# Group 0's top keys chosen, fetched and scored inside the early expert tiles; two sequences' expert sums and their QKV moved one group later

## The reference

```
x = x + haar_attention(ln(x))        # QKV, 3-level Haar transform, product, inverse, output matrix
x = x + ffn(ln(x))                   # "early" routed experts: top 2 of 8, hidden 256, relu^2
x = x + attention(ln(x))             # 16 heads of 8; per head three softmaxes, averaged:
    local : keys with |i - j| <= 128
    top   : the 128 keys with the highest (ln(x) @ Ws.T + bs) for this head
    global: the first 64 keys
x = x + ffn(ln(x))                   # "late" routed experts, same weights
```

## Time and profile before

| | us |
|---|---|
| median of 3 executions | 564.72 |
| profiled execution, its own time | 566.64 |
| its span in the profile | 564.9 |
| PE / DVE / ACT / POOL busy | 489.1 / 380.5 / 350.9 / 235.8 |

### The profile page before, as it was taken

One profiled execution on the slowest core, in us unless ns is written; L12 is line 12 of the kernel. 1 busy time (PEld: TensorE's weight loads), 2 busy tenths in 40 slices (PEclk: granted clock), 3 DMA queues, 4 the chain that ended last, 5 costly groups with the idle time before them and its releaser, 6 DMA issues.

```text
span 564.9 us, 12118 instructions
## 1 busy us (share of the span) xinstructions
PE 489.1 (87%) x3754; PEld 294.7 (52%) x3754; DVE 380.5 (67%) x1442; ACT 350.9 (62%) x835; POOL 235.8 (42%) x312
## 2 busy tenths in 40 slices
PE   7999899867767799997899989899989978789876
PEld 3577667646424344444455544444545423667665
DVE  4876886437777589897797777686888851334325
ACT  7577655766304767667657757577757556567643
POOL 3411164544474452242544245663543242445440
PEclk9999999998779899999999989999999999999989
DMA  7899012746120110000200002111010003656306
GB/s 225 294 358 306 2 42 73 258 171 227 39 63 9 43 45 13 10 15 15 63 19 16 15 14 64 29 26 31 14 33 17 25 31 109 238 168 213 125 15 185
DMA packets 52094, 51.65 MB, mean 91 GB/s; under 512 B 11811, under 2 KB 43689, under 8 KB 52032
## 3 DMA queue, kind: packets, MB, share of 16 engines
q1 hardware_dynamic: 46976, 44.52, 24.4%
q0 software_dynamic: 5056, 6.37, 4.5%
HBM read 12.11 MB, written 22.63 MB: 61 GB/s over the span
## 4 chain that ended last, share of the span: by engine, by line
PE 57%; DVE 18%; issue 10%; ACT 7%; DMA 4%; SPq 2%; another core or an unknown queue 1%; POOL 1%; DVEq 0%; ACTq 0%; POOLq 0%
PE BANK L1889 6%; PE BANK L1953 5%; PE BANK L1978 4%; PE BANK L1925 4%; PE BANK L2061 4%; PE BANK L1857 3%; PE BANK L1845 2%; PE BANK L1981 2%; PE BANK L1930 2%; PE BANK L1984 2%; PE BANK L2192 2%; PE BANK L1948 2%; PE BANK L1794 2%; DVE XN_c L1523 2%; PE BANK L1956 2%
## 5 line engine op out<-in xcount | busy, mean ns | idle before, releaser
L1166 ACT ACTIVATE PT<-BANK 128x256 f32<-128x256 f32 (+2 forms) x352 | 158.1, 492 | 97.0 <-PE BANK L1953 70.9
L746 POOL DMA_INDIRECT GOT<-kv_rows,CHOSEN x64 | 65.5, 1024 | 47.5 <-PE BANK L1953 25.2
L1523 DVE CUSTOM_DVE_ANT_0 XN_c<-BANK,BANDQ 128x384 f32<-128x384 f32 (+1 forms) x128 | 67.8, 530 | 12.4 <-PE BANK L1925 5.2
L1523 DVE CUSTOM_DVE_ANT_0 XN_a<-BANK,BANDQ 128x256 f32<-128x256 f32 (+1 forms) x128 | 56.7, 443 | 21.4 <-PE BANK L1925 17.3
L1528 DVE TENSOR_REDUCE QST<-BANK 128x4 f16<-128x512 f32 x64 | 44.3, 696 | 19.2 <-PE BANK L1930 13.2
L1978 PE MATMUL BANK<-PT,V 128*32 128x256 f32 (+1 forms) x512 | 49.2, 457 | 0.7 <-ACT PT L1166 0.6
L1889 PE MATMUL BANK<-XNT_ALL,W 128*128 128x512 f32 x96 | 46.7, 612 | 0.0
L798 POOL DMA_INDIRECT yt_late<-QKV,IDY_late x31 | 30.4, 980 | 33.6 <-DVE QKV L1388 23.4
L980 ACT ACTIVATE PT<-BANK 128x512 f32<-128x512 f32 x48 | 27.6, 598 | 24.5 <-PE BANK L1889 23.3
L1948 PE MATMUL BANK<-BANDK,IDB 128*128 128x256 bf16 x128 | 36.0, 282 | 7.4 <-ACT PT L1166 5.9
L766 POOL TENSOR_TENSOR SUM<-NRM 128x128 f32<-128x128 f32 x16 | 7.3, 458 | 80.0 <-DVE NRM L1544 79.8
(11 more groups left out here) (369 smaller groups left out, 1249.4 us busy)
## 6 DMA issues: line engine op xcount, KB each, us to landing
xs_late<-W SPq DMA_DIRECT2D x1, 6984.0 KB, 36.4
xs_early<-W SPq DMA_DIRECT2D x1, 4680.0 KB, 16.5
KZB<-W SPq DMA_DIRECT2D x16, 256.0 KB
KZC<-W SPq DMA_DIRECT2D x15, 256.0 KB
kv_rows<-KV SPq DMA_DIRECT2D x4, 768.0 KB
PT<-W SPq DMA_DIRECT2D x11, 256.0 KB
QKV<-xs_late SPq DMA_DIRECT2D x31, 72.0 KB
W<-w SPq DMA_DIRECT2D x2, 1024.0 KB, 8.2
```

What stands on the lines that cost most here:

```text
L746: nc.gpsimd.indirect_dma_start(GOT[g % 2][:, i, :], None, KV_ROWS[g // GROUPS][:, :], bass.IndirectOffsetOnAxis(ap=CHOSEN[:, c:c + 1], axi ...
L1166: nc.scalar.activation(PT[u % PT_RING][:, 0:w], P2_BANK[u % SCORE_RING][:, 0:w], ACT.Exp, scale=SCALE).then_inc(S["exp_done"], 1)
L1523: nc.vector.tensor_tensor_reduce(out=JUNK[v % 2][:, 0:n], in0=P1_BANK[v % SCORE_RING][:, 0:n], in1=BANDQ[:, off:off + n], scale=1.0, scala ...
```

## The change

- **Key choice.** `ROUNDS_TILE` has 5, 3 and again 5 steps a tile instead of 2 and 3, so that all 47 stand at tiles 4 to 15; `turn_orders(0)` and `row_choice(0)` come at tile 16, now through bank 7; `turn_keys(0)` and `chosen_keys(0)` at tile 20.
- **Row numbers for the scatter.** `early_id` leaves DVE; POOL makes each number itself, right before the DMA that uses it, after the wait for `tile_y`.
- **Fetch.** POOL issues group 0's four fetches after tiles 16 and 17, two each, and copies them after tile 18. Group 1's fetch still follows the 23rd tile and the wait for all result DMAs. `global_values(0)` moves ahead of the tiles.
- **SP.** The spreads of groups 0 and 1 are issued in halves after the loads of tiles 14, 15, 17 and 18; the rows of K and V are stored after load 16 instead of load 12; `spread_top(0)` comes before the results' loads.
- **First scores.** 18 of group 0's 22 first-pass units (all but the top ones) stand at tiles 14 to 21. The tiles' result bank is one instead of two (bank 4 is now a score bank). 29 of the 37 fillers go.
- **Moved into the groups.** The adds and statistics of sequences 2 and 3 go to (0, 8) up to (1, 1) (`SUM_C`), `rstd` to POOL's group 1, the normalisations to (1, 4) and (1, 10), their turns and the score of the second key choice from group 0 to group 1, its steps from groups 1 to 5 to groups 2 to 6, its last part from (5, 7) to (6, 13). The eight QKV products, which stood in groups 1, 1, 2, 2, 3, 3, 4 and 6, stand in groups 2, 2, 2, 3, 3, 4, 5 and 6.
- **Group 8.** Its chosen keys are turned at (7, 5) instead of (6, 13), and its first pass has the top units last (as groups 0 and 1), no longer spread. POOL issues its fetches at units 15 to 21 of group 6, and all of group 9's fetch at the start of its group 7.

```diff
-MORE_ROUNDS = {(g, u) for g in range(1, 5) for u in range(0, UNITS, 2)} | {(5, u) for u in (0, 2, 4)}
+MORE_ROUNDS = {(g, u) for g in range(2, 6) for u in range(0, UNITS, 2)} | {(6, u) for u in (0, 2, 4)}
-ROUNDS_TILE = {i: 2 if i < 12 else 3 for i in range(4, NT_EARLY - 1)}
-ROWS_TILE, STORE_TILE = 7, 12
+ROUNDS_TILE = {i: 3 if 7 <= i < 12 else 5 for i in range(4, 16)}
+ROWS_TILE, STORE_TILE = 7, 16
+SPREAD_TILE = {14: (0, 0), 15: (0, 1), 17: (1, 0), 18: (1, 1)}
+ORDERS_TILE, GATHER_TILE, KEYS_TILE = 16, (16, 17), 20
+FIRST_TILE = 14
+SUM_C = {(0, 8): (2, 0), (0, 11): (2, 1), (0, 14): (2, 2), (0, 17): (3, 0), (0, 20): (3, 1), (1, 1): (3, 2)}
-NORMS_C = {(0, 4): 2, (0, 7): 3}
+NORMS_C = {(1, 4): 2, (1, 10): 3}
-SEL_GROUP, SEL_AT = 5, 7
+SEL_GROUP, SEL_AT = 6, 13
+LATE_GATHER = (15, 17, 19, 21)
...
+def first_scores(i):
+    return range(min(TOP_W, 9 * (i - FIRST_TILE) // 4), min(TOP_W, 9 * (i - FIRST_TILE + 1) // 4)) if i >= FIRST_TILE else range(0)
...
-        D_BANK = {"early": BANK[3:5], "late": BANK[3:4]}
+        D_BANK = {"early": BANK[3:4], "late": BANK[3:4]}
...            # POOL, tile_out
                 pool.wait_ge(R[w.tag]["tile_y"], n + 1)
+                i = n if w is EARLY else slot
                 if w is EARLY:
-                    pool.wait_ge(R[w.tag]["tile_id"], n + 1)
+                    nc.gpsimd.tensor_scalar(IDY["early"][:, i:i + 1], XT_IN["early"][n % IN_RING][:, D + 1:D + 2], float(UNUSED), None,
+                                            ALU.add).then_inc(R["early"]["tile_id"], 1)
+                    pool.wait_ge(R["early"]["tile_id"], n + 1)
...            # POOL, the tiles
             for n in range(NT_EARLY):
                 tile_out(EARLY, n)
                 if n == ROWS_TILE:
                     key_rows(0)
+                if n in GATHER_TILE:
+                    half = n - GATHER_TILE[0]
+                    pool.wait_ge(S["sel_done"], 1)
+                    gather(0, range(half * PAIR, (half + 1) * PAIR))
+                elif n == GATHER_TILE[-1] + 1:
+                    gathered(0)
             for slot in range(Y_RING):
                 pool.wait_ge(Y_OUT["early"][slot], 16 * slot_count(EARLY, slot))
-            global_values(0)
-            pool.wait_ge(S["sel_done"], 1)
-            gather(0)
-            gathered(0)
             gather(1)
-            rstd("c", 2)
-            rstd("c", 3)
             gathered(1)
             gather(2)
...            # POOL, at the start of group 7
+                if g - 1 == SEL_GROUP:
+                    gathered(2 * GROUPS)
+                    gather(2 * GROUPS + 1)
+                    gathered(2 * GROUPS + 1)
...            # DVE, the tiles
             for i in range(NT_EARLY):
-                early_id(i)
                 if QKV_TILE <= i < QKV_TILE + T + 1:
                     c_add(1, i - QKV_TILE)
                 picks(0, ROUNDS_TILE.get(i, 0))
-            picks(0, PICKS)
-            both_orders(0)
...
+                if i == ORDERS_TILE - 1:
+                    picks(0, PICKS)
+                    both_orders(0)
+                if i == ORDERS_TILE:
+                    row_choice(0)
+                if i == KEYS_TILE:
+                    chosen_keys(0)
+                maxima(first_scores(i))
...            # PE, the tiles
+                if i == ORDERS_TILE:
+                    turn_orders(0)
+                if i == KEYS_TILE:
+                    turn_keys(0)
+                for w in first_scores(i):
+                    p1(0, w)
```

166 lines of the change are left out of this document (81 added, 85 removed).

## The result

The changed kernel takes 568.12 us (median of 20 runs, 565.54 to 572.7); the kernel before, run beside it, 565.68 (20 runs). The ratio is 1.0053, 95% interval 1.0031 to 1.0075: slower by half a per cent. The forecast was 556.7, and the range up to 564.5 does not hold the time. The profiled execution has 568.62 us, its span 566.8 (564.9).

What follows compares the result with a forecast made beforehand. The groups run at their limit on PE and DVE, so gain lies only before the first groups; -11.5 - 2.5 + 1.5 + 2 + 2.5 = -8.0 us, 556.7 us on the median of 564.7, range 548.5 to 564.5.

Steps and rivals of the forecast that it cites:

- steps 1 to 3: From the key choice to PE's turn of group 1's keys at (0, 2): that turn comes 11.5 us earlier.
- steps 5 to 7: Groups 1 to 7: work moved in and late service of groups 8 and 9 cost +1.5, +2 and +2.5 us.
- step 4: Rest of group 0 after (0, 2): 19.5 us instead of 22.0, -2.5, with DVE the fullest engine.
- Step 1: Key choice at the tiles: both orders written at about 138.8 us instead of 149.0.
- PE's idle stretch: At tile 15: PE idle 3 to 6 us, its fourth first-pass score waiting for DVE's first maximum.
- Step 2: From the choice to group 0: scatters of 1.65 us, group 0 could begin 15.8 us earlier, at 158.9.
- Step 3: At (0, 2): PE waits 4.3 us for group 1's keys, behind four scatters; (0, 2) at 165.3, -11.5 us.
- Rival A: At the tiles: scatters of 2.45 us make POOL the clock; kernel slower, 568.2 us; chance 9%.
- The rule cited from the Trainium skill: Group 0: two-SBUF-input DVE instructions hold off POOL's SBUF reads; four adds cost POOL 1.6 us, at most 2.8.
- B: Rival, in the groups: they hide the work given them, steps 5 to 7 give +1, 551.7 us; chance 18%.
- C: Rival, in the groups: full charge and clock low after each wait, step 4 +1, 561.2 us; chance 14%.
- D: Rival, at the tiles: PE or late loads delay the choice or tile 16 to 144, 562.2 us; chance 9%.

Runs made afterwards that it cites:

- e14: Changed kernel with early tiles' down products alternating between two result banks up to tile 13; ratio to the kernel before 1.0063.
- e11: Changed kernel with row numbers a tile ahead, group 1's fetches before the last four scatters, dense second key choice, two result banks; ratio to the kernel before 0.9845.
- e2: Changed kernel with POOL making each row number one tile ahead of its scatter; ratio to the kernel before 1.0044.
- e6: Changed kernel, unchanged, measured again as reference for the follow-ups; 546.19 us, ratio to the kernel before 1.0087.
- e7: Kernel before with only the late half: work moved into the groups, group 0 still prepared behind the tiles; ratio to the kernel before 1.0027.
- e4: Changed kernel with second key choice dense over (2, 0) to (5, 4), groups 8 and 9 served as before; ratio to the kernel before 1.0018.
- e12: Changed kernel with numbers a tile ahead, group 1's fetches early, dense second choice, ten fillers before group 0's key turn; ratio to the kernel before 0.9866.
- e5: Kernel before the change, unchanged, measured again as reference for the follow-ups; 541.45 us.

## Why the prediction was wrong

The parts first. Up to group 8 the forecast is -8.0 us and the first pair has +5.4. Of these 13.4 us, 6.8 are lost by (0, 2), steps 1 to 3, and 7.2 in groups 1 to 7, steps 5 to 7; step 4 gives 0.5 back.

*Step 1, the choice.* Both orders written at 141.08, forecast 138.8. DVE adds the first QKV product at 121.67 in place of 117.88: 1.2 us of this are the later start of the trace, 2.6 the single bank, which makes PE late. The steps and additions behind it run faster than forecast (three steps in 1.49 us in place of 1.55) and win 1.5 back. What failed is "the scores are in at 110.01, as now" (111.74) and the 0.5 us for the single bank, which moreover is named in the step but not added in its sum. The bank costs 2.3 us of the choice (e14). PE's idle stretch is 3.7 us, at tile 17 and for a load, not for a score at tile 15. That it is harmless was not tried, but e11, the fastest kernel, has 3.93 there.

A reading that was off: the clock line of the earlier trace rows is below 9 in slices 10, 11, 12 and 14, that is from 127 to 169 us and from 184 to 198; slice 13 is at 9. No term of the sum hangs on it.

*Step 2, to group 0.* Forecast -15.8, measured -12.3. CHOSEN is 2.6 late (143.39 against 140.8). The first fetch is late by that and by 0.5 more, since POOL is still at a scatter (143.38 to 144.44), and the keys by 3.9, since two scatters at 2.11 stand between.

*Step 3, the step that failed.* The mechanism stands: PE waits at (0, 2) for group 1's fetch, behind four scatters and the landing of the last. Its size does not: 7.39 us in place of 4.3, and (0, 2) at 172.06, -4.7 in place of -11.5. The mis-sized term is "small operation 0.23, 0.3 until the DMA's start, 1.10: 1.65 us each". I took the 0.3 from DMAs that wait for nothing of POOL's own. It is 0.77, and the scatter 2.11. e2, the kernel with nearly my price (1.63), says what this term is worth. Counted from the dense additions, (0, 2) is 6.9 us earlier than before in e6 and 10.3 in e2, where 11.5 was forecast: 3.4 of the 4.6 us that are missing there. The first pair misses 6.8: 3.9 are there when group 0's keys are in hand (the late choice and two long scatters), four more long scatters add 2.0 and the last one's landing 1.2 (2.05 us of idle time in place of 0.9), and the landing and copies of the fetch give 0.3 back. Rival A had said that a scatter costs from 2.0 us on, and the wait it named is there in small, with a choice at 143 and not POOL at 148. It was given 9% because I tested its price on the operation alone. Its total, 568.2, is next to the measured 568.12 by luck: it had step 3 at 0 (measured -4.7) and groups 1 to 7 at +6 (measured +13.2).

What none of my steps saw: the late half by itself wins 10 us up to group 1's start, by taking the sums out of DVE's way (e7). My sum gave that gain and the early half's as one. Apart, they say that the early half has to beat 7.9 us won without it, and as built it does not.

*Step 4, the rest of group 0.* From (0, 2): 22.0 before, 18.97 after, -3.0. Forecast -2.5: the number is right, the reasons in part. PE starts at half clock after the wait, as said (0.50 from 172.06 to 175.00, 1.00 from 178 on). But DVE is not full (13.49 of 18.97), and PE's wait of 2.58 us for ACT, which I had put down to the normalisations, is there without them, at 183.22. The adds did not hold POOL's fetches: one begun at 191.63, beside an add from 191.68 to 192.36, took 1.01. An operation of POOL's that reads SBUF was held. L722 runs beside the add from 181.65 to 182.33:

```profile
181.82 1.52 POOL L722 TENSOR_TENSOR QST<-QKV,QST 128x512 f16<-128x512 f32 x1 [2.79 <-ACT KST L1108]
```

The same operation takes 1.15 us with no add beside it, at 187.19 in the kernel before, and 1.70 in e6 where both begin together (180.43 and 180.44). The rule cited from the Trainium skill ("SBUF — State Buffer", Who interferes with whom) is borne out for such an operation. The Trainium skill says in the same section that a probe did not see `tensor_tensor` stall a DMA. By the fetch of 1.01 the trace agrees. So the rule should not have been turned against the fetches, and the 1.37 of the earlier trace rows stays unexplained.

*Steps 5 to 7, mis-sized as well.* Forecast +1.5, +2, +2.5, in all 6. First trace: +4.5, +4.1, +4.6, in all 13.2, each over its upper bound (3, 3.5 and 4.5). Later measurement: +2.3, +3.7, +3.4 in e7, in all 9.4, and 10.5 in e6. In e7 each lies inside or just over its bounds, and all three on the dear side. So 3.4 us of the miss are there in both measurements. The other 3.8 are in the first pair alone, and their cause stays open (last section). In group 7 both waits that I named are there, for the spread keys, 1.66 and 1.05 us. I had let the waits overlap; they add. e4, where groups 8 and 9 are served as before, has group 7 back at 16.16, so their late service is its whole charge in the later measurement. For groups 1 to 6 the charge is measured (e7) and not taken apart: no run says what the normalisations, a QKV product or the steps cost alone.

*Rivals B to D.* B fails on the charge. Of C, the charge is there and the lasting low clock is not: the clock is back at 1.00 six us after the wait at (0, 2), and step 4 comes out at -3.0, not at +1. Fillers ahead of group 0's keys bring nothing that can be told (e12); at (0, 2) none were tried. D's late choice is there in small (143.4 against 144).

*The rest.* The sum, -11.5 - 2.5 + 6, becomes -4.7 - 3.0 + 13.2 = +5.5 at group 8 (5.4 by the times themselves, 333.01 against 327.58). The end is 3.5 less late in the first pair of traces, not in the later one (e6: 1.1 us more behind group 8 than e5).
